# Second FFN product of the last super-tile: its last four chunks added tile by tile, with residual and rotation behind each tile

## What is computed

```python
x = _ln(src) * (1.0 + scale) + shift                  # scale, shift from the time step
scores = q @ k / sqrt(32) + attention_bias            # 16 heads, masked keys out
x = x + (softmax(scores) @ v) @ Wo + bo
h = _ln(x) * g2 + beta2
ff = _gelu2(h @ W1 + b1) @ W2 + b2                    # _gelu2(z) = z * sigmoid(1.702 z), D_FF = 2048
x = x + ff
# per group of four features, with the angles of the batch:
out = [x0*ct + x1*st, -x0*st + x1*ct, x2*cp + x3*sp, -x2*sp + x3*cp]
```

## Time and profile before

| | us |
|---|---|
| median of 3 runs | 3511.86 (3510.07 to 3513.74) |
| profiled execution, own time | 3513.55 |
| its span, first to last instruction | 3511.9 |
| mean granted TensorE clock | 0.990 of 2.4 GHz |
| TensorE matmul busy | 3415.5 (97% of the span) |
| VectorE, ScalarE, GpSimd busy | 2484.8, 1885.7, 2084.0 |

### The profile page before, as it was taken

How to read it: one execution, slowest core, us unless ns; L and a number is a source line. 1 busy time by engine, 2 the same in 40 slices (tenths; PEclk the granted TensorE clock), 3 DMA queues, 4 the chain that set the end, 5 groups by cost and what they waited for, 6 DMA issues and landing times.

```text
span 3511.9 us, 60955 instructions
## 1 busy us (share of the span) xinstructions
PE 3415.5 (97%) x18338; PEld 1940.6 (55%) x18338; DVE 2484.8 (71%) x4176; ACT 1885.7 (54%) x2541; POOL 2084.0 (59%) x646
## 2 busy tenths in 40 slices
PE   8999799999999999999999999998899999999997
PEld 3444466666666666666666666665344444444443
DVE  5666599999999999999999999997333343342331
ACT  3222388888888888888888888885111111111110
POOL 0000499999899999999998999995211211220100
PEclk9999899999999999999999999999999999999999
DMA  8999999999999999999999999999311220220100
GB/s 286 340 339 339 359 364 349 346 346 353 396 345 344 352 351 348 394 349 350 348 350 366 375 351 345 349 348 325 83 35 38 72 55 17 72 67 4 48 12 12
DMA packets 288702, 906.20 MB, mean 258 GB/s; under 512 B 93344, under 2 KB 93344, under 8 KB 211360
## 3 DMA queue, kind: packets, MB, share of 16 engines
q1 hardware_dynamic: 240272, 811.43, 64.3%
q10 hardware_dynamic: 45840, 86.00, 6.9%
q0 software_dynamic: 2560, 8.39, 0.6%
HBM read 763.12 MB, written 142.61 MB: 258 GB/s over the span
## 4 chain that ended last, share of the span: by engine, by line
PE 85%; DVE 1%; DMA 1%; issue 0%; ACT 0%; SPq 0%; POOL 0%; DVEq 0%; ACTq 0%
PE b_T L765 27%; PE bank_ctx L788 14%; PE scores L731 14%; PE scores L1302 13%; PE b_T L1312 9%; PE bank_ctx L1312 3%; PE scores L1283 3%; PE scores L737 1%; DMA penb<-in_L_cond_b 1%; PE scores L1243 0%; PE scores L1292 0%; DVE probT L1150 0%; PE scores L1257 0%; ACT penb L1048 0%; DVE stats_c L1141 0%
## 5 line engine op out<-in xcount | busy, mean ns | idle before, releaser
L590 POOL TENSOR_TENSOR ring<-ring,penb 128x1856 f32<-128x1856 f32 x512 | 1903.9, 3756 | 504.1 <-DMA penb<-pen_scratch 418.4
L685 ACT ACTIVATE ring<-ring,low 128x2048 f32<-128x2048 f32 x512 | 1029.0, 2010 | 317.9 <-DVE low L654 317.9
L765 PEld LDWEIGHTS b_T<-ident,ring 128*128 128x128 f32 x8192 | 889.7, 141 | 432.7 <-DVE probT L638 429.5
L765 PE MATMUL b_T<-ident,ring 128*128 128x128 f32 x8192 | 1091.2, 276 | 5.2 <-DVE probT L638 4.5
L654 DVE CUSTOM_DVE_ANT_0 ring<-scores,ring 128x1024 f32<-128x1024 f32 x512 | 627.2, 1225 | 177.0 <-PE scores L731 154.1
L638 DVE COPY probT<-b_T 128x512 f32<-128x512 f32 x1024 | 702.1, 686 | 3.9 <-PE b_T L765 3.8
L654 DVE CUSTOM_DVE_ANT_0 ring<-scores,ring,low_part 128x1024 f32<-128x1024 f32 x512 | 652.6, 1275 | 0.4
L731 PE MATMUL scores<-keys,queries 128*128 (+1 forms) x2048 | 620.8, 424 | 21.3 <-DMA queries<-q_rows 16.9
L788 PE MATMUL bank_ctx<-probT,values 128*32 128x512 f32 x4096 | 545.3, 605 | 0.2 <-ACT ctxp L701 0.2
L695 ACT COPY probT<-b_T 128x512 f32<-128x512 f32 x1024 | 537.8, 575 | 0.5 <-PE b_T L765 0.5
L1015 POOL TENSOR_TENSOR keys_again<-keys_again,values 128x512 f32<-128x512 f32 x32 | 40.4, 1264 | 787.4 <-DVE values L1232 787.4
(11 more groups left out here) (127 smaller groups left out, 1912.2 us busy)
## 6 DMA issues: line engine op xcount, KB each, us to landing
ring<-in_fside_Bx16xSxS SPq DMA_DIRECT2D x512, 1024.0 KB, 7.5
keys<-k_rows SPq DMA_DIRECT2D x64, 1024.0 KB, 8.4
values<-v_heads ACTq DMA_DIRECT2D x128, 256.0 KB, 6.3
queries<-q_rows SPq DMA_DIRECT2D x128, 256.0 KB, 8.0
ctx_scratch<-ctxp ACTq DMA_DIRECT2D x128, 256.0 KB, 6.6
penb<-ctx_scratch SPq DMA_DIRECT2D x120, 256.0 KB, 4.7
k_rows<-part_hi SPq DMA_DIRECT2D x64, 256.0 KB, 3.3
k_rows<-part_lo SPq DMA_DIRECT2D x64, 256.0 KB, 3.4
```

Source lines behind the costliest of these rows:

```text
L590: nc.gpsimd.tensor_tensor(ring[:, j, 0:POOL_MASKED], ring[:, j, 0:POOL_MASKED], penb[:, j, 0:POOL_MASKED], ALU.add).then_inc(masked, 1)
L685: nc.scalar.activation(ring[:, k, :], ring[:, k, :], ACT.Exp, bias=low[:, k:k + 1], scale=-1.0, accum_out=column(sums_all, trip, k)).then_ ...
L765: last = nc.tensor.transpose(turn_bank(slot, n)[:, c * P:(c + 1) * P], ring[:, slot, at:at + P], ident[:])
```

## The change

In the last super-tile down(0) to down(11) stay as they are. The last four chunks, 12 to 15, are no longer added chunk by chunk: at steps f = 14 and 15 TensorE makes only up(14) and up(15), at f = 16 nothing, and at f = 17 it waits for all of `hidden` and then goes tile by tile, four chunks each, counting `down_done` once after each tile. VectorE waits for the count of one tile, adds the residual of that tile and rotates it, then goes to the next. The other super-tiles are as before.

```diff
@@ phase_c
+    LAST_BY_TILE = 4
@@ vector, ffn and late
-            if f == FB + 1:
+            if f == FB + 1 and not (isinstance(u, int) and u == NU - 1):
                 dve.wait_ge(down_done, u * FB + FB + 4)
                 for t in range(QT):
-                    nc.vector.tensor_tensor(y[:, t, :], acc[t], of(x2, u)[:, t, :], ALU.add).then_inc(acc_read, 1)
+                    add_rest(u, t)
+
+        def add_rest(u, t):
+            nc.vector.tensor_tensor(y[:, t, :], acc[t], of(x2, u)[:, t, :], ALU.add).then_inc(acc_read, 1)
 
         def late(u, t):
             if t < QT:
+                if isinstance(u, int) and u == NU - 1:
+                    dve.wait_ge(down_done, u * FB + FB - LAST_BY_TILE + t + 5)
+                    add_rest(u, t)
                 dve.wait_ge(acc_read, u * QT + t + 5)
@@ tensor, ffn
-            if f >= 2:
-                k = f - 2
+            k = f - 2
+            by_tile = isinstance(u, int) and u == NU - 1
+            if 0 <= k < (FB - LAST_BY_TILE if by_tile else FB):
                 pe.wait_ge(hid_ready, u * FB + k + 5)
@@
                 last.then_inc(down_done, 1)
+            if by_tile and k == FB - 1:
+                pe.wait_ge(hid_ready, u * FB + k + 5)
+                for t in range(QT):
+                    for k in range(FB - LAST_BY_TILE, FB):
+                        last = nc.tensor.matmul(acc[t], hidden[:, k % 4, t * P:(t + 1) * P], w2[:, k, :], start=False, stop=(k == FB - 1))
+                    last.then_inc(down_done, 1)
```

## The result

The changed kernel takes 3505.05 us (median of 12 runs, 3502.99 to 3507.23), the kernel before 3512.94 (median of 12, 3510.07 to 3515.63). The ratio is 0.9977, 95% interval 0.9969 to 0.9985: 7.9 us or 0.22% faster. The profiled execution has a span of 3501.3 us and an own time of 3502.99.

The account below looks back on a forecast made before the run. TensorE bounds the kernel, so only the tail behind it can gain: 14.20 - 4.15 = 10.05 us gained, 1.79 given back for the pause, 8.26 net, from 3511.86 to 3503.6 us. Range 3501.0 to 3507.4.

Parts of the forecast that it names:

- TensorE, order: Last super-tile: 32 records move behind up(15), none added or removed; up(15) starts right after up(14), 3.43 us earlier.
- The new wait: TensorE behind up(15): idle until VectorE finishes hidden(15), a pause of 1.79 us, bounds 1.67 and about 2.1.
- VectorE and GpSimd per tile: From the end of a tile's product through addition, rotation and GpSimd's addition to its store's issue: 4.15 us.
- What hides the first three tiles: A tile comes every 3.43 us, VectorE needs 2.51 and GpSimd 2.22, so no delay accumulates; store margin 1.2.
- The collision: Tile 3's residual addition on VectorE falls inside GpSimd's addition of tile 2; taken as 0, 0.22 us if held.
- The reading that extends the block to every VectorE instruction: GpSimd's addition would hold even VectorE's addition with one input in PSUM, at tile 3; 0.22 us.
- The stretch behind the last issue: From the last store's issue to the span's end, landing and closing of the program: stays 5.46 us.
- a fifth of its forecast's chance: Of the forecast's 84%, a fifth was given to a measured gain below 7.0 us, which is 0.2%.
- A clock that falls: TensorE's clock halves in the pause, slowing all 32 records behind it: 13.7 us more, time 3517.3; chance 3%.
- No overlap: Tail behind TensorE stays 14.20 us and the pause comes on top: time 3513.7; chance 2%.
- A late store: Tile 1's store lands after 4.7 us instead of 2.4, tile 3's rotation waits: time 3504.7; chance 6%.
- A larger restart: TensorE's pause is 1 to 2 us longer than the bound: time 3504.6 to 3505.6; chance 5%.

Follow-up runs that it names:

- e1: Changed kernel, but in tile 0 TensorE waits for each of chunks 12 to 15 of hidden separately; 3502.87 us, ratio to before 0.9968.
- e2: Changed kernel, but VectorE waits for all four tiles ahead of the first residual addition; 3512.22 us, ratio to before 0.9997.
- e5: Changed kernel with two last chunks made tile by tile instead of four (LAST_BY_TILE = 2); 3506.28 us, ratio to before 0.9980.
- e7: e1 plus VectorE adding rot_a and rot_b of the very last tile and the SP queue issuing that one store; 3500.14 us, ratio to before 0.9963.
- e9: e7 with all four stores of the last super-tile issued from the SP queue; 3499.72 us, ratio to before 0.9965.
- e8: Kernel before, with only the four stores of the last super-tile issued from the SP queue; 3510.96 us, ratio to before 0.9993.
- e4: Kernel before, but the last super-tile's tiles 2 and 3 rotate into buffers of their own, so none waits for a store; 3512.52 us, ratio 1.0000.

## Why the prediction was right

**The sum.** The prediction had 8.26 us; the trace shows 8.12 to the last issue and 8.16 to the end, the medians 7.9. Its terms:

- *TensorE, order.* As said: down(11) and then 16 records without a gap.
- *The new wait.* 1.73 to the first record, where 1.79 was predicted. The 0.06 for a slower start shows in the stream instead: the first 24 records take 10.40, not 10.30. From the end of up(15) to the last record it is 15.56 against the predicted 15.52. e1 shows that it is a full term of the path.
- *VectorE and GpSimd per tile.* 4.15 predicted, 3495.88 - 3491.63 = 4.25 measured. The 0.10 is L1237 at 0.46 instead of 0.35: it started at 3492.56, while GpSimd issued tile 2's store (3492.37, 0.56 long). I had only looked at the collision with GpSimd's addition, not with its store. One tile earlier the two started as far apart, and it was the issue that took 0.10 more, off the path:

```profile
3488.94 0.66 POOL L1018 DMA_DIRECT2D out<-keys_again  x1 [0.30 <-POOL keys_again L1016]
3489.13 0.36 DVE L1237 TENSOR_SCALAR keys_again<-probT,cosines 128x256 f32<-128x256 f32 x1
```

- *What hides the first three tiles.* Right: 1.1 us idle ahead of each later addition, and no wait for a store. e2 shows the size of this cover when all of it is taken away, 8.3 us by the issue. In e5, with half of it, TensorE's end to the last issue takes 7.4 us instead of 4.25, of which its earlier end gives 1.8 back.
- *The collision.* The addition of tile 3 began at 3491.84, inside GpSimd's from 3490.82 to 3492.07, and took 0.69. The term is 0, as the earlier trace rows had it. By what the prediction takes from the Trainium skill, "Advanced Engine Details and Errata" (Mode Summary under VectorE Performance Modes), it is 0 as well. The reading that extends the block to every VectorE instruction is refuted by the 0.69.
- *The stretch behind the last issue.* 5.42 against 5.46. I took it as fixed, which is right for this change. But I called it the landing and the closing of the program, and e7 to e9 show that half of it hangs on who issues the last store and waits for it.

**The time.** 3503.6 was forecast and 3505.05 measured. Of the 1.45, the median of before accounts for 1.08: it was 3511.86 in three runs and 3512.94 in twelve. The gain accounts for the remaining 0.37: 7.89 by the medians against 8.26. The trace shows only 0.10 to 0.14 of that; the rest is within the scatter of the two medians.

**The rivals.** *A clock that falls*: not at 1.73 nor at 3.52 us; at 5.34 it fell, for 3.1 us. The direction of that rival was real, its place and its price were not: 13.7 us needs all 32 records at the low level. *No overlap*: e2 is that case, at 43.82 to the end against 43.69. The prediction priced it at 1.8 us slower than before, by leaving the tail at 14.20; measured it was 12.51, because VectorE goes tile by tile and rotates the first tile ahead of the other three additions: the first store is issued 4.16 behind TensorE's end instead of 5.85. *A late store*: didn't come, and the median landing of the four stores of the changed kernel's last super-tile was 2.3. *A larger restart*: didn't come.

**0.2%.** The measured 0.22% lies over 0.2%, with an interval from 0.15% to 0.31%. So a gain is shown, and that it is over 0.2% is not: that the medians fell on this side of it was in part luck. The prediction had said so, with a fifth of its forecast's chance for a gain below it.

## What to carry over

At the end of a program, ask of the last wave of work what can be finished piece by piece while the main engine still runs; the gain is the old tail less the tail of one piece, less what the new order costs the main engine. A piece must last longer on the main engine than on the slowest engine behind it (here 3.43 against 2.5; at 1.72 the old collisions and waits came back), and a wait that stood ahead of all pieces belongs ahead of the first use only. Measure such a change from a fixed instruction near the end, since the rest of the program scatters by more than the gain.

## What was unexpected of the hardware

- After the issue of GpSimd's last store the span went on for 5.4 to 5.5 us, of which 2.3 were the landing; after SP's, for 2.4 to 2.7 us, of which 2.0 were the landing. With all four stores on SP instead of GpSimd, the kernel before ended 2.4 us earlier by the trace (e8), which the runs don't tell from no change. What the 3.1 us behind GpSimd's landing are, no row here shows.
- VectorE and GpSimd hold each other in either direction: a VectorE instruction of 0.33 took 1.34 (e4), and a GpSimd addition of 1.25 took 2.52 (e8). VectorE's instruction had the same lead in both, 0.18 and 0.19 us. GpSimd's issue of a store and a VectorE instruction that began 0.19 us after it cost one of the two 0.1 us: VectorE (0.46 instead of 0.35, the issue 0.56) or the issue (0.66, VectorE 0.35), with both outcomes in the changed kernel.
- A pause of TensorE of 3.52 us cost its length; one of 5.34 us cost 3.1 us on top, at a clock of 0.50 for some 6 us behind it.
